# Attention over a graph: one-hot selections made once and kept in memory, indices written further ahead, GpSimd waiting on TensorE itself

## The reference, cut to what matters

```
out = segment_sum(norm[:, None] * h[src], dst)
```

```
ft = (feat @ W).reshape(n, 8, 32)
e = leaky_relu(a1[src] + a2[dst]);  m = segment_max(e, dst)
ex = exp(e - m[dst]);  alpha = ex / segment_sum(ex, dst)[dst]
out = segment_sum(ft[src] * alpha[:, :, None], dst)
```

## Time and profile before

| | us |
|---|---|
| median of three runs | 12359.25 |
| the profiled execution | 12387.94 |
| its span, first to last instruction | 12386.2 |
| conv1 | about 2972 |
| conv2 | about 2974 |
| attention | about 3664 |
| busy: TensorE matmul / VectorE / ScalarE / GpSimd | 5829.3 / 4864.5 / 1572.1 / 5048.9 |

### The profile page before, as it was taken

One profiled execution on the slowest core, in us unless ns is written; L12 is line 12 of the kernel. 1 busy time (PEld: TensorE's weight loads), 2 busy tenths in 40 slices (PEclk: granted clock), 3 DMA queues, 4 the chain that ended last, 5 costly groups with the idle time before them and its releaser, 6 DMA issues. The chain is left out here.

```text
span 12386.2 us, 140297 instructions
## 1 busy us (share of the span) xinstructions
PE 5829.3 (47%) x23283; PEld 4370.6 (35%) x23284; DVE 4864.5 (39%) x15561; ACT 1572.1 (13%) x3470; POOL 5048.9 (41%) x5288
## 2 busy tenths in 40 slices
PE   5543333333343222222223899555555555555239
PEld 3432222222233222222223455444444444444126
DVE  7622222222232222222223422355555555555731
ACT  0100000000000000000000432322222222222411
POOL 0035555555533555555553000244444444444231
PEclk5555555555555555555555699766666666666559
DMA  1100000000001000000000000223223232232320
GB/s 35 42 24 19 19 19 19 19 19 19 19 12 52 10 10 10 9 9 10 10 10 7 10 19 18 93 85 86 83 86 86 83 87 84 86 86 86 113 79 19
DMA packets 380624, 523.08 MB, mean 42 GB/s; under 512 B 148358, under 2 KB 277694, under 8 KB 380348
## 3 DMA queue, kind: packets, MB, share of 16 engines
q0 software_dynamic: 198928, 349.25, 11.0%
q1 hardware_dynamic: 180460, 170.51, 4.4%
q10 hardware_dynamic: 960, 0.00, 0.0%
HBM read 450.68 MB, written 68.72 MB: 42 GB/s over the span
## 5 line engine op out<-in xcount | busy, mean ns | idle before, releaser
L665 POOL DMA_INDIRECT conv_rows<-table,conv_idx x3328 | 3147.9, 946 | 3295.9 <-ACT conv_idx L653 2340.6
L718 PE MATMUL conv_pm<-conv_rows,conv_sel 128*128 x7040 | 1829.9, 416 | 4173.3 <-issue 2839.3
L718 PEld LDWEIGHTS conv_pm<-conv_rows,conv_sel 128*128 128x128 f32 x7040 | 1612.5, 324 | 4390.7 <-issue 4390.6
L1509 POOL DMA_INDIRECT att_rows<-ft_rows,att_idx x1760 | 1677.1, 953 | 3105.7 <-ACT att_idx L1523 2585.8
L707 DVE TENSOR_TENSOR acc<-acc,conv_pm 128x64 f32 (+1 forms) x3520 | 716.4, 204 | 3037.5 <-issue 2506.2
L1685 PE MATMUL att_pm<-att_rows,att_sel 128*128 128x264 f32 x3520 | 1409.4, 543 | 511.1 <-issue 393.0
L691 DVE TENSOR_SCALAR conv_sel<-iota,edges,edge_w 128x128 f32<-128x128 f32 x3528 | 1020.9, 355 | 1275.0 <-issue 1243.4
L1685 PEld LDWEIGHTS att_pm<-att_rows,att_sel 128*128 128x128 f32 x3520 | 882.7, 268 | 883.9 <-issue 676.8
L1821 DVE TENSOR_TENSOR sums<-sums,att_pm 128x264 f32 x1760 | 749.3, 426 | 217.0 <-PE att_pm L1685 163.7
L653 ACT ACTIVATE conv_idx<-sources 128x8 int32 x416 | 86.7, 208 | 5713.7 <-PE conv_pm L718 4913.0
L1764 DVE TENSOR_TENSOR_SCAN att_my<-att_fl,att_cc,att_mx 128x128 f32<-128x128 bf16 x110 | 53.2, 484 | 1390.2 <-ACT att_cc L1577 1390.2
(11 more groups left out here) (342 smaller groups left out, 6189.0 us busy)
## 6 DMA issues: line engine op xcount, KB each, us to landing
att_bc<-places SPq DMA_DIRECT2D x110, 512.0 KB
conv_rows<-table,conv_idx POOLq DMA_INDIRECT x3328
att_rows<-ft_rows,att_idx POOLq DMA_INDIRECT x1760
ft_rows<-proj_ft SPq DMA_DIRECT2D x25, 544.0 KB
x_normal<-elu_xr SPq DMA_DIRECT2D x25, 514.0 KB
x_spilled<-x_rows SPq DMA_DIRECT2D x25, 512.0 KB
elu_xg<-x_spilled SPq DMA_DIRECT2D x25, 512.0 KB
x_first<-x SPq DMA_DIRECT2D x6, 2048.0 KB
```

Source lines behind the costliest of these rows:

```text
L665: pool.indirect_dma_start(out=rows[:, k, :], out_offset=None, in_=table, in_offset=bass.IndirectOffsetOnAxis(ap=idx[:, k:k + 1], axis=0)). ...
L718: ins = nc.tensor.matmul(pm[q][:, i, :], sel[:, q * QUAD + i, :], rows[:, ds(slots[i], 1), :].rearrange("p a c -> p (a c)"), start=True, s ...
L1509: pool.indirect_dma_start(out=rows[:, k, :], out_offset=None, in_=K.ftd, in_offset=bass.IndirectOffsetOnAxis(ap=idx[:, k:k + 1], axis=0)). ...
```

## The change

In conv1 ScalarE also makes the unweighted selection of every step, as relu(1 - |place - iota|), and stores it to DRAM, 512 KB for a section of eight steps, through its own DMA queue; the 12 sections that are left after the last gather (there are 220 sections of steps and 208 of tiles) come at the end. The index ring of both convolutions shrinks from 128 to 32 tiles. In the attention VectorE's `hots` are gone; SyncE loads each quad's four selections (256 KB) from DRAM as soon as TensorE has finished the same quad of the block before. The ring of indices grows from 6 to 18 sections, and GpSimd, beside the indices, waits for TensorE's count of sums itself before it gathers into a section's slots.

```diff
-def graph_sum(nc, K, name, table, acc, C, x=None):
+def graph_sum(nc, K, name, table, acc, C, x=None, keep=False):
+    AHEAD = 4 * SECT
-        idx = ph.sb("idx", [P, SLOTS], I32)
+        idx = ph.sb("idx", [P, AHEAD], I32)
+        hot = ph.sb("hot", [P, 2, SECT, P]) if keep else None
         @block.scalar
...
+            def ones_of(b, j):
+                first, half, section = b * AHEAD + j * SECT, j % 2, b * (AHEAD // SECT) + j
+                act.wait_ge(stored[half], (b * (AHEAD // SECT // 2) + j // 2) * 16 + 16)
+                for k in range(SECT):
+                    ins = act.activation(hot[:, half, k, :], K.iota[:, :], ACT.Abs,
+                                         bias=K.edges[:, 1, ds(first + k, 1)], scale=-1.0)
+                ins.then_inc(apart, 1)
+                act.wait_ge(apart, section + 1)
+                act.activation(hot[:, half, :, :], hot[:, half, :, :], ACT.Relu, bias=K.ones[:, 0:1], scale=-1.0
+                               ).then_inc(made, 1)
+                act.wait_ge(made, section + 1)
+                act.dma_start(K.seld[ds(section * 2, 2)].rearrange("q p f -> p q f"),
+                              hot[:, half, :, :].rearrange("p (q i) n -> p q (i n)", i=QUAD)).then_inc(stored[half], 16)
...
-            with act.Fori(0, TURNS) as b:
-                for j in range(SLOTS // SECT):
+            with act.Fori(0, TB * P // AHEAD) as b:
+                for j in range(AHEAD // SECT):
                     act.wait_ge(mm_done, t + (UNROLL - LAG + 1))
-                    act.wait_ge(arrived, t + SECT)
+                    act.wait_ge(arrived, t + (SECT + LANES - AHEAD))
                     act.activation(idx[:, j * SECT:(j + 1) * SECT], K.srct[:, ds(t, SECT)], ACT.Copy
                                    ).then_inc(idx_ready, 1)
+                    if keep:
+                        ones_of(b, j)
+            if keep:
+                for b in range(TB * P // AHEAD, STEPS // AHEAD):
+                    for j in range(AHEAD // SECT):
+                        ones_of(b, j)
+                for h in range(2):
+                    act.wait_ge(stored[h], 16 + STEPS // SECT // 2 * 16)
 def attention(nc, K):
+    AHEAD = 2 * LONG
-        idx = ph.sb("idx", [P, SLOTS], I32)
+        idx = ph.sb("idx", [P, AHEAD * SECT], I32)
         @block.sync
+            def selections(n, q):
+                sp.dma_start(sel[:, q * QUAD:(q + 1) * QUAD, :].rearrange("p i n -> p (i n)"),
+                             K.seld[ds(n * NQ + q, 1)].rearrange("a p f -> p (a f)")).then_inc(sel_loaded[q], 16)
...
+            def body(b, more, most, further):
                 if most:
                     sp.wait_ge(m_ready, b + 2)
                     flags(b + 2)
+                for q in range(NQ):
+                    if q == 2 and further:
                         sp.wait_ge(t_ready, b + 3)
                         places(b + 3)
+                    if more:
+                        sp.wait_ge(mm_done, b * SEGS + (q + 1) * QUAD)
+                        selections(b + 1, q)
         @block.gpsimd
-            def section(turn, j):
-                pool.wait_ge(idx_ready, turn * SECTS + j + 1)
+            def section(n, j, free=None):
+                pool.wait_ge(idx_ready, n + 1)
+                if free is not None:
+                    pool.wait_ge(mm_done, free)
                 pool.sem_inc(taken, 1)
...
+            with pool.Fori(0, laps) as lap:
+                for j in range(AHEAD):
+                    section(lap * AHEAD + (SECTS + j), (SECTS + j) % AHEAD, lap * (AHEAD * SECT) + (j + 1) * SECT)
         @block.scalar
                     act.wait_ge(mm_done, b * SEGS + (k + 1) * SECT)
-                    if not isinstance(turn, int) or 2 * b + k + SECTS < STEPS // SECT:
-                        take(b * 2 + (k + SECTS), (2 * i + k) % SECTS)
+                    if not isinstance(turn, int) or 2 * b + k + AHEAD < STEPS // SECT:
+                        take(b * 2 + (k + AHEAD), 2 * i + k)
         @block.tensor
             def factor(n):
                 pe.wait_ge(p_ready, n + 1)
-                pe.wait_ge(sel_ready, n * NQ + 1)
             def sums(b, i, q, k0=0, k1=QUAD):
                     pe.wait_ge(weighed, b * NQ + q + 1)
-                    pe.wait_ge(sel_ready, b * NQ + q + 1)
+                    pe.wait_ge(sel_loaded[q], b * 16 + 16)
         @block.vector
-            def hots(n, q):
-                s, at = n * SEGS + q * QUAD, q * QUAD
-                tt(sel[:, at:at + QUAD, :], count.unsqueeze(1).to_broadcast([P, QUAD, P]),
-                   K.edges[:, 1, ds(s, QUAD)].unsqueeze(2).to_broadcast([P, QUAD, P]), ALU.is_equal
-                   ).then_inc(sel_ready, 1)
...
-                hots(b, 2)
-                hots(b, 3)
...
+        K.seld = dram("selections", [STEPS // QUAD, P, QUAD * P])
-                graph_sum(nc, K, "conv1", K.t1, K.acc1, CH1)
+                graph_sum(nc, K, "conv1", K.t1, K.acc1, CH1, keep=True)
```

More of the change, by code:

```diff
@@ L635, in graph_sum @@
     with Phase(nc, name) as ph:
-        idx = ph.sb("idx", [P, SLOTS], I32)
+        idx = ph.sb("idx", [P, AHEAD], I32)
         rows = ph.sb("rows", [P, SLOTS, C])
+        hot = ph.sb("hot", [P, 2, SECT, P]) if keep else None
+        stored = [ph.sem(f"stored{h}") for h in range(2)]
         sel = ph.sb("sel", [P, RING * QUAD, P])
@@ L640, in graph_sum @@
         gathered = [ph.sem(f"gathered{k}") for k in range(LANES)]
-        idx_ready, taken, sel_ready, mm_done, added, arrived, zeroed, x_loaded = (
-            ph.sem(x_) for x_ in ("idx_ready", "taken", "sel_ready", "mm_done", "added", "arrived", "zeroed", "x_loaded"))
+        idx_ready, taken, sel_ready, mm_done, added, arrived, zeroed, x_loaded, apart, made = (
+            ph.sem(x_) for x_ in ("idx_ready", "taken", "sel_ready", "mm_done", "added", "arrived", "zeroed", "x_loaded",
+                                  "apart", "made"))
         block = ph.block()
@@ L1436, in attention @@
         pm = [ph.ps(f"pm{i}", [P, 512]) for i in range(QUAD)]
-        pwi = ph.ps("pwi", [P, 2, P])
-        pw, count = pwi[:, 0, :], pwi[:, 1, :]
+        pw = ph.ps("pw", [P, P])[:, :]
         pxr = ph.ps("pxr", [P, 3, P])
@@ L1490, in _ @@
             places(2)
-            def body(turn, i, more, most):
-                b = block_of(turn, i)
+            def body(b, more, most, further):
                 if most:
@@ L1496, in body @@
                     flags(b + 2)
-                    if not isinstance(b, int) or b + 3 < NB:
+                for q in range(NQ):
+                    if q == 2 and further:
                         sp.wait_ge(t_ready, b + 3)
                         places(b + 3)
-            blocks(sp, body)
+                    if more:
+                        sp.wait_ge(mm_done, b * SEGS + (q + 1) * QUAD)
+                        selections(b + 1, q)
+            with sp.Fori(0, NB - 3) as b:
+                body(b, True, True, True)
+            for b in range(NB - 3, NB):
+                body(b, b < NB - 1, b < NB - 2, False)
         @block.gpsimd
         def _(pool):
-            def section(turn, j):
-                pool.wait_ge(idx_ready, turn * SECTS + j + 1)
+            def section(n, j, free=None):
+                pool.wait_ge(idx_ready, n + 1)
+                if free is not None:
+                    pool.wait_ge(mm_done, free)
                 pool.sem_inc(taken, 1)
[L1508 to L1517, removed]
+                for k in range(SECT):
+                    at = j * SECT + k
+                    pool.indirect_dma_start(out=rows[:, at % SLOTS, :], out_offset=None, in_=K.ftd,
+                                            in_offset=bass.IndirectOffsetOnAxis(ap=idx[:, at:at + 1], axis=0)
+                                            ).then_inc(gathered[j % SECTS], 16)
+            for n in range(SECTS):
+                section(n, n)
+            laps = (STEPS // SECT - SECTS) // AHEAD
+            with pool.Fori(0, laps) as lap:
+                for j in range(AHEAD):
+                    section(lap * AHEAD + (SECTS + j), (SECTS + j) % AHEAD, lap * (AHEAD * SECT) + (j + 1) * SECT)
+            for n in range(SECTS + laps * AHEAD, STEPS // SECT):
+                section(n, n % AHEAD, (n - SECTS + 1) * SECT)
         @block.scalar
@@ L1583, in weights @@
                 act.activation(pw, df[:, 0:P], ACT.Exp).then_inc(p_ready, 1)
-            act.activation(count, K.iota[:, :], ACT.Copy).then_inc(counted, 1)
-            for j in range(SECTS):
+            for j in range(AHEAD):
                 take(j, j)
@@ L1825, in _ @@
             own.did(dve.memset(K.acc[:, :, :, :], 0.0))
-            hots(0, 0)
-            hots(0, 1)
             local(0)
@@ L1859, in body @@
                 where = places(b, 2)
-                if more:
-                    hots(n, 0)
                 add(b, 2, where)
@@ L1874, in body @@
                     weigh(n, i + 1, 2)
-                    hots(n, 1)
             blocks(dve, body)
```

19 lines of the change are left out of this document (12 added, 7 removed).

## The result

The changed kernel takes 12423.0 us (median of 5, 12420.48 to 12432.60), the kernel before beside it 12358.81: ratio 1.0052, 95% interval 1.0040 to 1.0065. It is 64 us slower; I had forecast 31 us faster. The profiled spans are 12386.2 and 12430.9 us.

The account below looks back on a forecast made before the run. Each stage's period was taken as gather burst, 3.1 us, and the chain to GpSimd's release. Terms -37 + 11 - 5 + 0 = -31 us gave 12328 us from 12359.25; range 12150 to 12440.

Parts of the forecast that it names:

- The hold: Some 6 us into a gather burst other engines' sequencers slow and TensorE's signals are held, until 3.1 us after it.
- the attention's period: Attention, per block: 19.87 us of burst, 3.1 us, then the chain to GpSimd's release; 32.94 us together.
- The port: Attention: hots might hold the port VectorE shares with GpSimd; removing them could give up to 146 us, but counted 0.
- GpSimd's own wait, -37: Attention: releasing GpSimd without ScalarE's index write saves 0.35 us in each of 107 bursts, 37 us (22 to 48).
- TensorE's wait +11: Attention: one more wait per quad, only quad 1's on the chain, costs 0.1 us a block, 11 us (0 to 25).
- last blocks -5: Attention's last three blocks, without gathers: removing hots shortens VectorE's chain by 5 us (2 to 8).
- loads 0: Attention: SyncE's loads of selections, four times 256 KB a block, are hidden and cost 0.
- conv1, 0: conv1: ScalarE's added 3.9 us a section fits beside the gathers and costs 0, upper bound 165 us.
- My rival: conv1: ScalarE ends its second section late, so GpSimd starts later; 50 to 165 us lost, time 12380 to 12490, chance 0.29.

Follow-up runs that it names:

- own wait: Kernel before with only the attention's indices 18 sections ahead and GpSimd waiting for the sums itself; 12320.66 us, ratio 0.9968.
- scalar_releases: Changed kernel with the attention's indices again six sections ahead and ScalarE's index write releasing GpSimd; 12455.72 us, ratio 1.0089.
- the making alone: Kernel before plus own wait, with conv1's ScalarE making the selections but storing none, hots still on VectorE; 12425.82 us, ratio 1.0050.

## Why the prediction was wrong, step by step

- **The hold and the attention's period: right** on the chips I had the trace from. The period is burst, 3.2 us and the same chain; `hots` beside it and in the hold were worth next to nothing (VectorE 235 us less busy in all where I had said 290, since it is 30 us busier in conv1, and with own wait already in place the attention's stretch went from 3567.5 to 3563.0 us). The port that the prediction weighed by the Trainium skill is not held by `hots`: of the gathers of the kernel before, 88 begin while one of them runs, and none of these takes over 0.95 us. But I had read sixteen gathers only, and the trace has longer ones. 81 of the attention's 1760 take over 1.0 us, up to 1.41, and every one of them begins inside a VectorE scan whose two tensor operands both lie in SBUF; `hots`, the adds and the weighings have one operand in PSUM. Such a gather ends 0.76 us after the scan does (with 0.25 us of the scan left it takes 1.01, with 0.66 left 1.41); with 0.15 us or less left it takes its 0.95. Where the two begin within 0.05 us of each other, it is in some cases the gather that takes 0.95 and the scan that takes up to 0.08 us more. So it is in scalar_releases, where 68 gathers are long:

```profile
9497.98 0.71 DVE L1793 TENSOR_TENSOR_SCAN att_ro<-att_th,att_rv 1x272 f32<-1x272 f32 x1 [0.28 <-issue]
9498.04 1.42 POOL L1554 DMA_INDIRECT att_rows<-ft_rows,att_idx  x1 [0.30 <-issue]
```

It costs little: in the kernel before 14 us over the whole attention, in the changed kernel, where no gather is over 1.0 us, nothing. Sixteen gathers take 19.87 us at the median before, 19.70 changed and 20.16 in scalar_releases.
- **GpSimd's own wait, -37: right.** 35 us alone (23 to 54 by its interval), 46 when undone; 0.35 us in the block shown. That 0.35 was chosen between bounds of 0.21 and 0.45, so a part of the hit is luck.
- **TensorE's wait +11, last blocks -5, loads 0:** the +11 is not seen (the stretch from 3567.5 to 3563.0 us, which holds it, went down by 5); the last blocks lie behind the last gather, where the rest of the program got 3 us shorter, too little to tell; the loads are shown to be hidden.
- **conv1, 0: the step that failed.** The term measured +90 us. I asked only whether ScalarE would be done in time: "Even if it made no step in the hold, it would need 3.9 us of these 4. So 0." It was done 18 us early. I had not asked who else works in the last half microsecond before the hold. VectorE's four selections ended the kernel before's quick stretch at +5.6 to +6.7 with nothing to spare; 0.2 us later they fall into the hold, cost slow operations themselves, and a step of TensorE's is left for afterwards. My rival named the right stage and, by chance, a range that holds the 90 us, but its mechanism (ScalarE late after the hold) is wrong: GpSimd's release waits for TensorE, and ScalarE has idled 18.47 us. Its premise was wrong too: ScalarE is not slowed in the hold like the others. Between +6.8 and +21 us of conv1's bursts three quarters of the register operations of TensorE and of VectorE take over 0.5 us (before), but of ScalarE's none with the making alone (of 203) and 152 of 404 in the changed kernel, most of them at its loop's end, behind the second store.
- The sum: -35 for own wait, +90 for conv1, 0 to -5 for the rest of the attention is 50 to 55. The profiled spans differ by 45, the medians by 64; between these two numbers lies that the profiled execution of the kernel before was 29 us above its median and that of the changed kernel 10. The 9 to 14 us by which the medians exceed the sum are not explained.

Shown: making costs the 90 us, storing at most some 20 and perhaps nothing; the shorter ring costs nothing; without a hold none of them costs anything that shows. Seen side by side, not shown as a cause: the kernels with the cost are those in which VectorE's selections are late, 54 to 96% of the periods against 5 to 22%. Not shown: why ScalarE's making delays VectorE there, and what the hold is. The Trainium skill (Runtime: NRT & Kernel Launch, "Instruction fetch mechanics") says that a taken branch outside the prefetched pages stalls an engine until its target is fetched. With the making alone VectorE's first slow operation of a burst is in 33 of 91 periods the one behind its loop's branch (698 ns at +5.03 us in the burst that begins at 1545.91) and in 12 the branch itself, which would fit; but operations far from any branch are as slow later in the hold, and no run here shows a fetch.

## What to carry to other kernels

Where other engines run against a moment at which all slow down, ask of added work on an idle engine not whether it ends in time, but whose last operations before that moment it can push over it; the price is a step, not a share. An edit of idle time can have opposite signs on two chips (0.9929 and 1.0052 here), so the kernel before must be profiled beside each experiment, and a rule read from one trace is a rule of that chip until seen elsewhere. Of several experiments on a disputed cost, leaving out each half (stores, making) told most, while moving a piece changed the course of the periods and told little. And two runs of a program can differ by an event that comes in a few blocks only (the bursts of 8 here), so a profiled execution must be held against its own median.

## What was not expected of the hardware

- The same kernel takes 9284 us on some chips and 12356 on others, at equal gather durations (0.95 us). On the latter, during bursts of gathers by GpSimd, sequencer operations of TensorE and VectorE take 0.7 us instead of 45 ns, nearly one at a time over the two together (23 of them between +5.8 and +22 us of the burst at 1026.43), and the convolutions take 2865 instead of 2081 us. ScalarE's are mostly spared: in the changed kernel's burst at 1037.63 its first eight Abs take 2.44 us before the hold and the second eight 2.45 in it.
- The slow operations end at about +22 us whatever is done before; only their begin moves (+4.4 to +6.1 on average).
- Stores of 512 KB lengthen other engines' register loads from 0.56 to 0.98 us at most (on chips without the hold); it cost nothing measurable there.
- A gather that begins inside a VectorE scan with both tensor operands in SBUF ends 0.76 us after that scan and so takes up to 1.43 us instead of 0.95; beside `hots`, the adds and the weighings, with an operand in PSUM, it takes 0.94 to 0.96.
- In three blocks of one execution the attention went on in bursts of 8 gathers and 24.9 us a block instead of 32.5. What starts or ends that is not shown.
